# An attention and mixture-of-experts block on one core: scatters, routing and shared pairs in another order between attention and the routed tiles

## The reference

```
mod = silu(c) @ wmod                       # shift, scale and gate, twice
h = layernorm(x) * (1 + ca) + sa
x = x + ga * attention(h)                  # 32 heads, window of 8, masked softmax
h = layernorm(x) * (1 + cb) + sb
scores = sigmoid(h @ gate_w.T)             # 16 experts
topv, topi = top_k(scores, 2); topv = topv / topv.sum()
y = mlp(h, sw1, sw2, sw3)                  # the shared expert, 352 wide
y = y + sum over experts e of weight_e * mlp(h, w1[e], w2[e], w3[e])   # 176 wide
mlp(h, w1, w2, w3) = (silu(h @ w1.T) * (h @ w3.T)) @ w2.T
x = x + gb * y
```

## Time and profile before

| | |
|---|---|
| runs (3), median | 410.24 us |
| lowest and highest | 409.18 and 412.09 us |
| the profiled execution, its own time | 408.21 us |
| its span, first to last instruction | 406.4 us |
| mean granted clock of TensorE | 0.96 |
| PE, DVE, ACT, POOL busy | 357.5, 284.5, 157.3, 120.9 us |

### The profile page before, as it was taken

How to read it: one execution, slowest core, us unless ns; L and a number is a source line. 1 busy time by engine, 2 the same in 40 slices (tenths; PEclk the granted TensorE clock), 3 DMA queues, 4 the chain that set the end, 5 groups by cost and what they waited for, 6 DMA issues and landing times.

```text
span 406.4 us, 12935 instructions
## 1 busy us (share of the span) xinstructions
PE 357.5 (88%) x5187; PEld 266.9 (66%) x5187; DVE 284.5 (70%) x632; ACT 157.3 (39%) x374; POOL 120.9 (30%) x149
## 2 busy tenths in 40 slices
PE   7876988999998999878768696699999999998994
PEld 4555877888787787766535264477777777774463
DVE  2758496979788898999833623568777777761597
ACT  1142253544545463401323100345555555551440
POOL 6300004040404030121587173034343444442000
PEclk9999899999999999988995989879999999999999
DMA  8736355564646343424252023123333333201943
GB/s 278 223 92 179 91 135 147 148 182 115 177 104 186 93 147 92 145 83 144 57 206 104 26 104 106 54 79 117 118 113 118 113 116 82 68 10 59 316 143 103
DMA packets 56124, 50.55 MB, mean 124 GB/s; under 512 B 22768, under 2 KB 50841, under 8 KB 55938
## 3 DMA queue, kind: packets, MB, share of 16 engines
q1 hardware_dynamic: 43360, 30.17, 26.0%
q10 hardware_dynamic: 8914, 11.13, 8.8%
q0 software_dynamic: 3792, 8.43, 5.9%
HBM read 28.70 MB, written 20.87 MB: 122 GB/s over the span
## 4 chain that ended last, share of the span: by engine, by line
PE 70%; DVE 15%; issue 6%; DMA 3%; POOL 2%; ACT 2%; ACTq 1%; SPq 0%; DVEq 0%; POOLq 0%
PE bank L1508 11%; PE bank L1523 11%; PE bank L1384 8%; PE bank L1337 6%; PE bank L1272 6%; PE bank L1464 6%; PE bank L1310 3%; PE bank L1319 3%; PE bank L1291 3%; PE bank L1516 3%; PE bank L1491 3%; PE bank L1352 2%; DMA first_region<-wmod 2%; DVE region L870 2%; PE bank L1330 2%
## 5 line engine op out<-in xcount | busy, mean ns | idle before, releaser
L555 POOL DMA_INDIRECT yrows<-second_region,sloti x47 | 46.2, 984 | 77.6 <-ACT second_region L760 76.0
L1384 PE MATMUL bank<-xT_region,sw 128*128 128x512 f32 (+1 forms) x96 | 48.2, 655 | 3.8 <-DVE second_region L998 3.8
L1523 PE MATMUL bank<-w,second_region 88*128 x188 | 50.3, 391 | 1.2 <-DVE second_region L1135 1.2
L1508 PE MATMUL bank<-first_region,second_region 128*128 x141 | 43.4, 317 | 3.4 <-DVE second_region L1125 2.2
L1508 PE MATMUL bank<-region,second_region 128*128 x141 | 43.3, 316 | 0.0
L522 POOL DMA_INDIRECT hslots<-hxw,posi x32 | 31.7, 992 | 32.1 <-DVE posi L989 23.2
L1337 PE MATMUL bank<-region 128*32 128x16 f32 x2048 | 35.3, 212 | 3.1 <-issue 3.1
L1337 PEld LDWEIGHTS bank<-region 128*32 128x32 f32 x2048 | 35.1, 159 | 3.4 <-issue 3.4
L499 POOL TENSOR_TENSOR rstd2s<-ve,cft 128x2 f32<-128x2 f32 x8 | 5.7, 708 | 105.2 <-DVE ve L919 105.1
L1384 PEld LDWEIGHTS bank<-xT_region,sw 128*128 128x128 f32 (+1 forms) x96 | 18.5, 198 | 27.8 <-issue 22.2
L1523 PEld LDWEIGHTS bank<-w,second_region 88*128 88x128 f32 x188 | 33.1, 196 | 4.6 <-issue 1.7
(11 more groups left out here) (169 smaller groups left out, 683.0 us busy)
## 6 DMA issues: line engine op xcount, KB each, us to landing
region<-hslots SPq DMA_DIRECT2D x47, 129.0 KB
hslots<-zeros ACTq DMA_DIRECT2D x8, 516.0 KB
region<-vd SPq DMA_DIRECT2D x64, 64.0 KB, 2.2
region<-yrows SPq DMA_DIRECT2D x16, 256.0 KB, 6.0
modb<-moddram SPq DMA_DIRECT2D x8, 384.0 KB, 4.1
xs<-x SPq DMA_DIRECT2D x8, 256.0 KB, 3.9
vd<-second_region SPq DMA_DIRECT2D x8, 256.0 KB, 2.9
out<-xs SPq DMA_DIRECT2D x8, 256.0 KB, 2.1
```

The costliest lines, as they stand in the source:

```text
L555: gp.indirect_dma_start(yrows, bass.IndirectOffsetOnAxis(ap=sloti[:, s:s + 1], axis=0), yo[:, s % RING, :], None, bounds_check=TOPK * T - ...
L1384: last = pe.matmul(o[0:p], sw13[:, c, half * SI + f * P:half * SI + f * P + p], xT[:, c, g * GT * P:(g + 1) * GT * P], start=c == 0, stop= ...
L1508: last = pe.matmul(UP(s), parts[:, s % 2, m, c * P:(c + 1) * P], w13[c][:, bass.ds(experts[s], 1), :], start=m == c == 0, stop=m == EXACT ...
L1523: last = pe.matmul(YP(s), hT2[0:IH, s % 2, k, :], w2[:, k, bass.ds(experts[s], 1), :], start=k == 0, stop=k == 1)
```

## The change

Nothing is computed otherwise; instructions move. Five things change.

- POOL: four scatters of round 0 move from ahead of `rstd2(7)` to behind it (`EARLY`), and ahead of the fourteenth (i = 13) POOL waits until pair 3 is made on PE (`su_p` at 4).
- PE: `count(1)` stands ahead of all of pair 4 and no longer between its halves. Pairs 6 and 7 are made ahead of the routed tiles (`EXTRA`), and `up(0)` waits for the second of them to be consumed.
- DVE: `times_b(3)` moves ahead of `ranked(1)`. `times_b(6)` and `(7)` move ahead of the routed tiles, and the first four `goes_to` ahead of `less_high(0)`.
- ACT and DVE behind the tiles: four pairs remain there, in another order with `scaled_y` and `combine`.
- Buffers: `yo` and then the buffers of the routed tiles all lie behind those of the shared pairs, so the two no longer overlap.

```diff
 PIECES = ((), (0, 1), (2, 3), (4, 5), (6, 7), (8, 9), (10,), ())
+EXTRA = 2
...
+        last.at = late.at
+        yo = last.take("j d", (RING, D,))
...
         parts = last.take("j m t", (2, EXACT, C * P,), BF16)
...
         hT2 = last.take("j k t", (2, 2, P,))
-        last.at = late.at
-        yo = last.take("j d", (RING, D,))
...
-            EARLY = (4, 9)
+            EARLY = (4, 5)
+            REST = 13
...
             for i in range(EARLY[1], TOPK * ROUND[1]):
+                if i == REST:
+                    gp.wait_ge(su_p, 4)
                 place_rows(0, i)
...
-            for n in range(2, SK * AHEAD):
+            for n in range(2, SK * AHEAD + EXTRA):
                 silu_g(n)
...
             result(NS - 1)
-            silu_g(SK * AHEAD)
...
-            silu_g(7)
             silu_g(8)
             scaled_y(0)
+            silu_g(9)
             scaled_y(1)
-            silu_g(9)
             scaled_y(2)
+            silu_g(10)
             scaled_y(3)
-            silu_g(10)
             scaled_y(4)
+            silu_g(11)
             scaled_y(5)
-            silu_g(11)
             scaled_y(6)
             scaled_y(7)
...
             times_b(2)
+            times_b(3)
             ranked(1)
             new_tiles(1)
             placed(1)
-            times_b(3)
             behinds()
...
                 keep_shared(t)
+            for n in range(EXTRA):
+                times_b(SK * AHEAD + n)
             gates()
...
+            for s in range(RING):
+                goes_to(s)
             less_high(0)
...
             hidden(1)
-            for s in range(4):
-                goes_to(s)
...
-            times_b(6)
-            times_b(7)
+            times_b(8)
             for k in range(RING):
                 dve.wait_ge(put[k], 16 * len(range(k, NS, RING)))
-            times_b(8)
             combine(0)
...
             finish(1)
+            times_b(10)
             combine(2)
-            times_b(10)
             modulated_y(2)
...
             up_shared(3)
-            up_half(4, 0)
             count(1)
-            up_half(4, 1)
+            up_shared(4)
             up_shared(5)
...
-            pe.wait_ge(su_m, SK * AHEAD)
+            for n in range(EXTRA):
+                up_shared(SK * AHEAD + n)
+            pe.wait_ge(su_m, SK * AHEAD + EXTRA - 1)
...
             turn_rows(1)
+            pe.wait_ge(su_m, SK * AHEAD + EXTRA)
             up(0)
...
-            for n in range(SK * AHEAD, SK * GROUPS):
+            for n in range(SK * AHEAD + EXTRA, SK * GROUPS):
                 up_shared(n)
```

## The result

The changed kernel takes 394.81 us (median of 4 runs, 393.87 to 396.00), the kernel before 411.16 us (4 runs, the three shown above and one more, 409.18 to 414.83). The ratio is 0.9594, with a 95% interval of 0.9519 to 0.9669: 4.1% less time, where 400.4 us were forecast and 396.5 was the lower end of the range. The profiled execution took 396.0 us, with a span of 394.2 (before 406.4) and a mean clock of 0.974 (before 0.96).

The account below looks back on a forecast made before the run. It took PE, with 70% of the chain, as the bound, through idle gaps and half clock before the tiles. Terms -4.0 - 1.7 - 4.1 = -9.8 gave 398.4 profiled, plus 2.0 for the median: 400.4 us, range 396.5 to 406.

Parts of the forecast that it names:

- The head: Between attention and routed tiles: earlier norm, full PE clock and earlier count bring `down_shared` forward by 12.4 us.
- Root: `rstd2(7)` on POOL, with four fewer scatters ahead of it, starts at about 205.9 instead of 209.98: -4.1 us.
- chances: `chances(1)` starts at 214.4, after -4.1 from the root and -2.5 from PE running at full clock.
- `ranked`: `ranked(1)` on DVE starts at 220.4 against 228.50, -8.1 us in all, its count needing only the pick.
- `down_shared`: On PE, starts at 226.6 against 239.00 and keeps its 14.4 us, 4 of them waits; ends at 241.0.
- the first step: In the head: the inverse root `rstd2(7)` 4.1 us earlier, then 2.5 us from PE at full clock.
- the second: In the head: the second count no longer waits behind half of pair 4; `ranked(1)` reaches -8.1 us in all.
- Rival C: Better, 396: `down_shared`'s waits partly absent, POOL then setting `less_high(0)` at about 248, or no clock fall before the tiles; chance 0.15.
- POOL: Last scatter ends at 241.4, first row read by 246.8, 1.1 us ahead of PE; the rest costs nothing.
- A rule against this: DVE's copies might lock POOL's port during scatters laid beside the routing: +5.4 us by the rule, none by a trace row.
- The tiles: PE's wait for the fifth row load goes, -1.7 us; clock early in the tiles net nothing, bounds -2.7 and +2.6.
- The tail: Behind the routed tiles, four pairs instead of six and an earlier `combine(0)` on DVE: -4.1 us, bounds -1.5 and -4.5.

Follow-up runs that it names:

- y2: Kernel before with only `EARLY = (4, 5)`, one scatter instead of five ahead of `rstd2(7)`: 403.18 us, ratio 0.9855 to the kernel before.
- w1: Changed kernel with the four scatters back ahead of `rstd2(7)`: 404.94 us, ratio 0.9851 to the kernel before.
- w2: Changed kernel with `count(1)` back between the halves of pair 4 and `times_b(3)` behind the routing: 401.27 us, ratio 0.9755 to the kernel before.
- y1: Kernel before, unchanged, run once more for a second profile: 409.43 us (one run), kernel before 408.22.
- first batch: Four undos of single parts of the changed kernel, on one chip, without the changed kernel beside them: 410.36 to 417.11 us, kernel before 411.96.
- z2: Changed kernel without POOL's wait ahead of the fourteenth scatter, third batch: 394.33 us, kernel before 408.76.
- w3: Changed kernel with pairs 6 and 7 back behind the routed tiles: 401.00 us, ratio 0.9742 to the kernel before.
- y3: Changed kernel with the first four `goes_to` back behind `hidden(1)`: 399.82 us, ratio 0.9815 to the kernel before.
- v2: Changed kernel with `EARLY = (6, 7)`, no POOL rest, gates ahead of `times_b(6)`, three of four targets later: 394.10 us, ratio 0.9676 to the kernel before.
- x3: Changed kernel with pairs 6 and 7 back behind the routed tiles, first batch: 410.36 us, ratio 0.9965 to the kernel before.
- x4: Changed kernel without POOL's wait ahead of the fourteenth scatter, first batch: 416.03 us, ratio 1.0088 to the kernel before.
- x1: Changed kernel with nine scatters of round 0 again ahead of the last layer norm, first batch: 417.11 us, ratio 1.0116 to the kernel before.
- z1: The changed kernel itself once more, third batch: 396.10 us, kernel before 408.76.
- v0: The changed kernel itself once more, fifth batch: 397.53 us, ratio 0.9711 to the kernel before.
- v1: Changed kernel with `EARLY = (6, 7)` and no POOL rest: 395.56 us, ratio 0.9688 to the kernel before.

## Why the prediction was right or wrong

**Direction and places: right.** Every place at which it expected a gain gave one. The time forecast was 5.6 us too high. The same kernel took 396.10, 395.89 and 397.53 us in the later batches, so that 394.81 is its lowest median; which side of 396.5 it falls on is in part luck. The miss in the mechanism, below, stands in every trace.

**The head: right.** Root -4.1 (forecast -4.1), chances -7.0 (-6.6), `ranked` -8.8 (-8.1), `down_shared` -12.8 (-12.4). The clock stayed at 1.00 to 248. (A pair is 3.46 us by the prediction's own row, 20.77 / 6, and not 3.43; nothing hangs on it.) y2 and w1 show the first step by itself, w2 the second.

**The step that failed: "`down_shared` itself, 14.4 us with 4 us of waits for DVE's `keep_shared`, I leave as it is: end 241.0".** It takes 10.7 us in the changed kernel and, in y1, in the kernel before as well. Fourteen of the 19 traces have 10.7 us; the others are the one shown before and the four of the first batch. The 4 us in the earlier trace rows were not the price of `keep_shared`: y1 has the same code and no such wait, and the 0.99 us of "remote" in the row above points to the late signals of the first batch, on a small scale. That it is the same thing was not shown. From this step followed pairs 6 and 7 ending at 247.9 and `less_high(0)` at 250.4, the -4.0 for the start of the tiles. On the time axis of before's profile the pairs end at 243.8 and `less_high(0)` starts at 247.0: -7.4. Rival C named this ("the 4 us of waits in `down_shared` are partly absent") and what would then bind ("POOL then sets `less_high(0)`"), but gave it 0.15. I should have seen that the waits had no cause in the code: each `keep_shared` takes 0.42 us, a tile of `down_shared` 1.3.

**POOL: right, and it was the bound.** Forecast: last scatter at 241.4, first row at 246.8 at the latest, the rest free. Measured on the same axis: 241.4, first transpose 245.2, and z2 agrees that the rest, there, is worth nothing. But the 1.1 us of slack that I gave POOL's queue was against a PE chain 4 us too long; w3 shows that the queue, and not the pairs, sets the start.

**A rule against this: the cost did not come, the lock did, the other way round.** Of the 23 rows of scatters from 216 to 244 us in the changed kernel one is of 1.00 us and the others of 0.96, beside the routing as behind it; the 5.4 us are absent (last scatter +35.6, not +41). But DVE waited. One of its copies in the routing, in the changed kernel beside a scatter and in the kernel before in POOL's idle stretch:

```profile
226.00 0.38 DVE L989 COPY hxw<-rtop 128x6 f32<-128x6 f32 x1
...
232.09 0.17 DVE L986 COPY hxw<-rtop 128x6 f32<-128x6 f32 x1
```

The scatter beside the first ran from 225.40 to 226.40, and the copy ended with it, at 226.38. It is so wherever the traces have such a pair: the 25 copies, casts and scalar operations of DVE that began 0.52 to 0.63 us into a scatter all ended within 0.03 us of its end and took 0.34 to 0.43 us, where the same instructions elsewhere take 0.17 to 0.25; those that began up to 0.48 us into it ran at their own length. The Trainium skill ("SBUF — State Buffer", "Who interferes with whom") says that whoever issues first gets the port for the whole instruction and the other blocks. These rows agree with it for the last 0.4 us or so of a scatter. DVE pays 0.2 us, twice in the changed kernel's routing, and POOL nothing that matters.

**The tiles: larger than forecast in the two profiles shown, not shown to be mis-sized.** Forecast -1.7 for the fifth row load's wait and nothing for the clock; measured -3.4. The wait is 1.71 us in the execution before, 1.99 in y1 and 2.12 in y3, whose tiles take 112.4 us against 110.2 to 111.4 in four profiles of the changed kernel. The rest lies in the clock, which I called "net nothing". Before, 1.2 + 2.0 + 0.2 = 3.4 us' worth of clock is missing from 260 to 272 in the windows above, after it 0.7 + 1.0 = 1.7 from 248 to 256, some of it ahead of the first `up`. In w2 and v2, where it does not fall, the tiles take 109. But in y1 the kernel before has its tiles in 112.3 us instead of 113.6, so two profiles of one kernel differ by as much as the part in question; over all profiles the gain is 0.9 to 3.4 us, and the forecast lies within.

**The tail: right.** Forecast -4.1, measured -4.2 (-3.5 to -4.2 over all profiles of the two kernels), by its reason: `combine(0)` stands 3.5 us nearer to the last `down` and DVE does not wait afterwards. w3 undoes it and has 37.2.

**The sum.** -7.3 - 3.4 - 4.2 against -4.0 - 1.7 - 4.1: of the 5.1 us between them 3.3 come from the start of the tiles, the failed step, which all four profiles of the changed kernel show (first `up` at +42.6 to +42.9, against +49.7 and +50.1), and 1.7 from the tiles, which may be chance. Against that the profiled execution had its attention 2.7 us late, so that it took 396.0 and not the forecast 398.4; and the median lies 1.2 below it, where I had added 2.0. So 5.6 = 5.1 - 2.7 + 3.2, and the last two terms are the spread of executions and not of the mechanism.

## What to carry to other kernels

Where two chains lead to one place, work out the end of both without the waits for which the code gives no reason; the chain that has slack by the trace may be the one that binds. A wait whose duration does not follow from the instructions around it is to be looked up in a second profile of the same kernel before it is put into a sum or left in one. And an undo that costs more than the whole change is first a reason to run the changed kernel beside it again, on the same chip, before it is a reason for a theory. A wait that one engine shows in front of a step need not be what holds the step: y3 took DVE's waits for the row loads away, and the step came when it had come before.

## What the runs showed of the hardware

- In one batch, on one chip, four kernels had engines released long after the work that they waited for. The waits began while POOL issued indirect DMAs; the longest two, 14.9 us in x3 and in x4, ended 4.0 us after the last scatter. In x4 ACT took pair 5 at 248.56, 19.0 us after PE's last matmul of it (229.53). The same kernel took 394.33 us in a later batch, on another chip, and 416.03 there, the kernel before 408.76 and 411.96. What held the signals up, the chip or something else, stays open. The rest is no protection, since x1 to x3 had it; the changed kernel itself was never in that batch, so what it would take there was not measured.
- The same attention code ended at 204.8 in one profiled execution (z2) and at 210.3 in another (z1), both kernels being the same up to there. That is as much as the differences between v0, v1 and v2, and the reason to compare traces from the last variance on.
- The clock ahead of the tiles: in v0, where PE waited 1.41, 1.01 and 1.46 us between pair 7 and the first `up`, it fell to 0.57; in v1, with 0.65 and 2.67, to 0.50; in v2, with 0.53 and 1.84, and in w2, with one wait of 3.57 us behind unbroken work, it stayed at 1.00. In w3, behind 8.29 us of idle time, it was 0.50 until 256, through 4 us in which PE was busy throughout. It is not the same from one execution to the next: with the same waits to within 0.1 us the windows from 248 to 256 have 0.83 and 0.75 in the execution shown after the change and 0.57 and 0.57 in v0.
